# Context handed over turned, first query stacks taken straight from SBUF, and constant rows written by another engine

## The chip, the cores and the metric

The kernel runs on one core of one Trainium2 chip. The metric is the device time of one execution in microseconds (us). The engines are TensorE (PE, with its weight loads PEld), VectorE (DVE), ScalarE (ACT), GpSimd (POOL) and SyncE (SP), which here only issues DMAs; ACT issues a few as well.

## The reference, cut to what matters

A gated cross-attention block is followed by a mixture-of-experts block. There are B=8 batches of T=256 tokens with HID=512 features. The change touches the first half alone:

```python
# hidden = layernorm(x), ssm = ctx_2048, H=32 heads of D=16, HK=8 key heads, G=4
q = concat([ssm, hidden], -1) @ Wq          # 1024 -> 512
k, v = hidden @ Wk, hidden @ Wv             # 512 -> 128
sk, sv = ssm @ Wsk, ssm @ Wsv
scores = q . concat(sk, k) / 4 + alibi bias, masked to a window of 64 keys
x = x + tanh(g_xattn) * (softmax(scores) @ concat(sv, v)) @ Wo
```

## The kernel before, in words

All eight batches are worked through on the one core. Every float32 product is made as three fp32r products: a value is split into a high part (a copy by ACT, names ending in `_hi`) and a low part (value minus high part, names ending in `_lo`, by DVE or POOL), and `PASSES` multiplies hi.hi, lo.hi and hi.lo.

Attention is written as one software pipeline over `SLOTS`. A slot is one block of scores of one key head. A batch has 32 slots (`UNITS`), four to a group (key head) g. Each engine has its own instruction list for a slot, written out in a fixed order, and work of other batches is hung in at fixed offsets with `due(n, offset)`: an offset of -31 is slot 1 of the batch before.

For batch b the steps are: SP loads the rows of x and of the context (`load_rows`); DVE makes row statistics, POOL inverse roots (`x_roots`) and the normalised rows (by DVE for the first two batches). `prep(b, i)` turns 128 rows at a time with four TensorE transposes into a bank of `ps_proj`, i = 0, 1 for the context and 2, 3 for x; `prep_high` (ACT) and `prep_low` (DVE) split the turned block into `actT_hi`, `actT_lo`. `keys_values` and `queries` multiply these with the weights. The two banks of `ps_proj` are used in turn, in the order of `projections()`: a job waits (`take_bank`) until the job two before it has been emptied by DVE (`pj_done`). In the steady pipeline prep stands in slots 0 to 3, the key products in slots 5 and 6.

Scores are made from two stacks in SBUF, `k_stack` (KS) and `q_stack` (QS): their middle rows hold the three parts of keys and queries, their other rows constants for mask and bias, written once for each group by ACT (`key_rows_out`, `query_rows_out`, five instructions a group). Keys and queries reach the stacks through DRAM (`keep_k`, `keep_q`, then `stack_k`, `stack_q`); only for the first batch's groups 0 and 1 (`DIRECT`) do queries go from SBUF to SBUF (`stack_q_first`). `maxima` (DVE) takes row maxima, which are turned, copied and put into the query stack by a small DMA of ACT (`max_rows`); `scores_turned` then makes the turned scores 14 slots (`LAG`) after `scores`, ACT takes exponentials (`probsT`), and `times_v`, two DVE transposes, a POOL scaling (`o_normal`) and a product with Wo follow.

Before slot 0 stands an opening, written out by hand on each engine: the weights are loaded through an eight-part staging buffer (`weight(n)`, order `halves`: Wsk, four parts of Wq, Wk, four of Wq, Wsv, Wv, then four of Wo), split by ACT (`weights_high`) and by DVE or POOL (`weights_low`), and batch 0 is projected, with batch 1's keys. Batch 1's queries are made in slots 3, 6, 9 and 12 (`SECOND_Q`) and go into the same `qT` buffers, so that `q_high` of batch 1 waits for batch 0's `keep_q`. The probabilities lie over the staging buffer, so that `exponentials` of slot 18 waits for the last weight part.

After attention come router, shared expert and experts, which the change leaves alone.

Of the kernel before, what the change touches and what calls it, by code (L numbers as in the profile page):

```python
# [78 lines left out]
PREP, K_PROJ, Q_PROJ, V_PROJ = (-32, -31, -30, -29), (-27, -26), (-24, -22, -19, -16), (-7, -5)  # L79
# [7 lines left out]

DIRECT, FILL_ROWS, SECOND_Q = 2, {0: 3, 2: 4, 4: 5, 6: 6, 8: 7}, (3, 6, 9, 12)
# [33 lines left out]
def projections():  # L122


    order = [("prep", 0, i) for i in range(4)] + [("k", 0, 0)] + [("q", 0, r) for r in range(G)] + [("v", 0, 0)]
    order += [("prep", 1, i) for i in range(4)] + [("k", 1, 0)]
# [11 lines left out]
def build(nc, a, out):  # L138
# [21 lines left out]
    CTX = at("ctx_rows", 140 * KIB, [P, TB, HID])  # L160
# [5 lines left out]
    OT = {h: at(f"oT_{h}", (184 + n * 4) * KIB, [P, TB, HC, P], F32R) for n, h in enumerate(("hi", "lo"))}  # L166
    OB = at("o_blocks", 192 * KIB, [P, 2, T // 32, 2 * D])
# [87 lines left out]
    ones_set, tg_done, q_rows_set, k_rows_set = sem("ones_set"), sem("tg_done"), sem("q_rows_set"), sem("k_rows_set")  # L255
# [7 lines left out]
    k_in, max_in = ([sem(f"{n}_in{g}") for g in range(HK)] for n in ("k", "max"))  # L263
    q_in = [sem(f"q_in{p}") for p in range(PAIRED)]
    q_first = [sem(f"q_first{g}") for g in range(DIRECT)]
# [29 lines left out]
    ctx_t = a["ctx_2048"].rearrange("b (t p) d -> p b t d", p=P)  # L295
# [53 lines left out]
    def tile_columns(i):  # L349

        src, t = i // TB, i % TB
        return slice(None), slice(src * HC, (src + 1) * HC), slice(t * P, (t + 1) * P)
# [85 lines left out]
    def _(sp):  # L438
        sp.dma_start(CTX[:, 0], ctx_t[:, 0, 0]).then_inc(ctx_first, 16)
        sp.dma_start(CTX[:, 1], ctx_t[:, 0, 1]).then_inc(ctx_in, 16)  # L440

# [20 lines left out]
        def keep_q(b):  # L462
            sp.wait_ge(pj_done, passed("q", b, G - 1))
            for j, (part, _) in enumerate(PASSES):
                sp.dma_start(q_kept_d[b % 2, :, j], Q[part][:].rearrange("p i f r w -> p (i f r w)").bitcast(F32)
                             ).then_inc(q_kept, 16)

        def stack_k(b, g):
            sp.wait_ge(k_kept, 16 * PARTS * (b + 1))
            if b == 0:  # L470
                sp.wait_ge(pad_kept, 16)
                sp.wait_ge(k_rows_set, g + 1)
            else:
                sp.wait_ge(st_mm, (b - 1) * UNITS + NB * (g + 1))
            sp.dma_start(KS[DATA:FINE, g].rearrange("p i v w s -> p i (v w s)").bitcast(F32),
                         key_pairs(b % 2, g)).then_inc(k_in[g], 16)

        def stack_q_first(g):
            sp.wait_ge(pj_done, passed("q", 0, G - 1))
            sp.wait_ge(q_rows_set, 4 * (g + 1))  # L480
            for j, (part, _) in enumerate(PASSES):
                sp.dma_start(QS[DATA + j * D:DATA + (j + 1) * D, g].rearrange("p i f r w -> p (i f r w)").bitcast(F32),
                             Q[part][g * D:(g + 1) * D].rearrange("p i f r w -> p (i f r w)").bitcast(F32)
                             ).then_inc(q_first[g], 16)

        def stack_q(b, p):
            gs = slice(2 * p, 2 * p + 2)
            sp.wait_ge(q_kept, 16 * PARTS * (b + 1))
            if b == 0:
                sp.wait_ge(q_rows_set, 8 * (p + 1))  # L490
            else:
                sp.wait_ge(st_mm, (b - 1) * UNITS + 2 * NB * (p + 1))
# [24 lines left out]
        for p in range(DIRECT // 2, PAIRED):  # L517
            stack_q(0, p)
            for g in (2 * p, 2 * p + 1):
                stack_k(0, g)  # L520
            if p == DIRECT // 2:
                keep_k(1)
        for n in range(SLOTS):
# [42 lines left out]
            if s == 1:  # L566
                sp.wait_ge(q_kept, 16 * PARTS * B)
# [75 lines left out]
    def _(pool):  # L643
# [23 lines left out]

        def scale_outputs(n):
# [40 lines left out]

        link(pool.memset(half[:], -0.5))  # L710
        pool.memset(VA[:], 1.0).then_inc(ones_set, 1)
# [6 lines left out]
        for n in range(SLOTS):  # L718
            b = due(n, STATS[1] + 1, 2)
# [135 lines left out]
    def _(act):  # L855
# [4 lines left out]
        def key_rows_out(g):  # L860
            act.activation(KS[:, g].rearrange("p i v w s -> p i (v w) s"),
                           key_rows[:].rearrange("p v w -> p (v w)").unsqueeze(1).unsqueeze(3).broadcast_to(
                               [P, NB, 2 * W, 2]),
                           ACT.Copy).then_inc(k_rows_set, 1)

        def query_rows_out(g):
            for r in range(G):
                act.activation(QS[:, g, :, :, r, :],
                               onehot[:].rearrange("p (f w) -> p f w", f=2).unsqueeze(1).broadcast_to([P, NB, 2, HQ]),
                               ACT.Copy, scale=slopes[:, g, r:r + 1]).then_inc(q_rows_set, 1)  # L870

        def prep_high(b, i):
            act.wait_ge(prep_t, 4 * b + i + 1)
            act.activation(AT["hi"][tile_columns(i)], chunks(place("prep", b, i)), ACT.Copy).then_inc(prep_hi, 1)
# [8 lines left out]
        def q_high(b, r):  # L883
            if b >= 1 and r == 0:
# [1066 lines left out]
```

## Time and profile before

| | |
|---|---|
| median of 3 runs | 981.62 us (979.45 to 984.07) |
| the profiled execution's own time | 981.09 us |
| its span | 979.2 us |
| PE busy | 93% of the span |
| DVE, POOL, ACT busy | 58%, 49%, 42% |

The span is what the profile covers from the first to the last instruction; the execution's own time is 1.9 us longer. Busy shares are means over stages with different limits, so they don't tell by themselves which engine holds up the end.

### The profile page before, as it was taken

How to read it: one execution, taken by the hardware profiler on the slowest of the kernel's cores; microseconds unless marked ns; L12 is line 12 of the kernel's file. 1: busy time of each engine (PE TensorE's matmuls, PEld its weight loads, DVE VectorE, ACT ScalarE, POOL GpSimd, SP SyncE). 2: the span in 40 equal slices, each digit the busy share in tenths (PEclk: the TensorE clock that was granted, in tenths of full speed). 3: DMA queues.
4: the chain of work that ended last, by engine and by line, in shares of the span. 5: the costliest groups of instructions: out<-in, count | busy, mean ns of one | idle time of the engine just before them, and what ended most of it. 6: DMA issues, size and time to landing. Idle time of an engine off the chain costs nothing.

```text
span 979.2 us, 17727 instructions
## 1 busy us (share of the span) xinstructions
PE 911.4 (93%) x6744; PEld 778.0 (79%) x6744; DVE 568.9 (58%) x1123; ACT 408.4 (42%) x858; POOL 477.6 (49%) x525
## 2 busy tenths in 40 slices
PE   6869999999998999989998979889999999999998
PEld 6768989888888979777786857678888888888886
DVE  5447575766667574666223654855556565555657
ACT  4655444453535353454311423333444444344431
POOL 1123061513333150325122997726688887888841
PEclk9979999999999999999999989999999999999999
DMA  6695567474747464697010113441110201201026
GB/s 222 169 189 156 128 165 194 136 198 118 200 131 203 108 190 112 159 254 250 1 44 22 43 52 124 139 161 44 66 65 28 81 22 65 86 22 66 22 95 249
DMA packets 80422, 117.01 MB, mean 120 GB/s; under 512 B 6345, under 2 KB 49098, under 8 KB 79306
## 3 DMA queue, kind: packets, MB, share of 16 engines
q1 hardware_dynamic: 78592, 115.11, 41.3%
q8 instruction: 54, 0.88, 0.4%
q10 hardware_dynamic: 1746, 0.77, 0.4%
q14 instruction: 30, 0.25, 0.1%
HBM read 77.13 MB, written 37.81 MB: 117 GB/s over the span
## 4 chain that ended last, share of the span: by engine, by line
PE 75%; DVE 9%; POOL 6%; DMA 4%; issue 4%; ACT 2%; SPq 1%; ACTq 0%; DVEq 0%; POOLq 0%
PE ps_proj L1550 21%; PE ps_scores L1849 18%; PE ps_scoresT L1849 9%; PE ps_o L1661 5%; PE ps_scores L1629 4%; PE ps_proj L1849 4%; PE ps_scoresT L1648 4%; PE ps_scores L1550 3%; PE ps_scoresT L1550 2%; DMA q_stack<-max_rows 2%; DVE actT_lo L1185 2%; DVE neg_max L1220 2%; DVE o_blocks L1238 1%; DMA q_kept<-qT_hi 1%; PE ps_o L1550 1%
## 5 line engine op out<-in xcount | busy, mean ns | idle before, releaser
L1220 DVE TENSOR_REDUCE neg_max<-ps_scores 128x2 f32<-128x384 f32 (+1 forms) x256 | 128.8, 513 | 139.0 <-PE ps_scores L1629 137.1
L910 ACT ACTIVATE probsT<-ps_scoresT 128x512 f32<-128x512 f32 (+1 forms) x256 | 134.9, 542 | 144.7 <-PE ps_scoresT L1648 141.3
L1629 PE MATMUL ps_scores<-k_stack,q_stack 114*128 114x192 f32 (+1 forms) x512 | 105.4, 290 | 13.9 <-DVE neg_max L1220 9.2
L1108 ACT ACTIVATE part_sums<-ps_scores 128x512 f32<-128x512 f32 x96 | 57.4, 598 | 137.9 <-PE ps_scores L1849 137.9
L1648 PE MATMUL ps_scoresT<-q_stack,k_stack 116*128 116x256 f32 x448 | 104.2, 304 | 6.7 <-DMA q_stack<-max_rows 4.6
L1629 PEld LDWEIGHTS ps_scores<-k_stack,q_stack 114*128 114x128 f32 x512 | 81.0, 195 | 27.8 <-DVE neg_max L1220 17.9
L673 POOL TENSOR_TENSOR o_normal<-o_blocks,inv_sums 128x128 f32<-128x128 f32 x64 | 25.7, 402 | 147.0 <-DVE inv_sums L1240 147.0
L796 POOL TENSOR_TENSOR w_expert_lo<-w_sums,w_expert_hi 128x256 fp32r<-128x256 f32 x64 | 64.2, 1015 | 45.8 <-ACT w_expert_hi L1039 45.8
L808 POOL TENSOR_TENSOR big<-big,basis 128x512 f32<-128x512 f32 x56 | 77.5, 1401 | 14.9 <-DVE basis L1494 14.9
L1648 PEld LDWEIGHTS ps_scoresT<-q_stack,k_stack 116*128 116x128 f32 x448 | 71.6, 194 | 9.8 <-DMA q_stack<-max_rows 5.2
L679 POOL TENSOR_TENSOR oT_lo<-oT_raw,oT_hi 128x256 fp32r<-128x256 f32 x32 | 23.5, 736 | 111.2 <-ACT oT_hi L919 111.2
L1550 PE MATMUL ps_proj<-actT_hi,wq_hi 128*128 128x256 f32 x224 | 65.0, 290 | 0.0
L1550 PE MATMUL ps_proj<-actT_hi,wq_lo 128*128 128x256 f32 x224 | 64.2, 287 | 0.0
L1550 PE MATMUL ps_proj<-actT_lo,wq_hi 128*128 128x256 f32 x224 | 64.2, 287 | 0.0
L1485 DVE TENSOR_TENSOR basis<-part_sums,silu_gate 128x512 f32<-128x512 f32 x32 | 24.2, 756 | 68.3 <-ACT silu_gate L1116 68.3
L1661 PE MATMUL ps_o<-probsT,v_ones 128*32 128x128 f32 (+1 forms) x2048 | 63.3, 265 | 0.5 <-issue 0.5
L1661 PEld LDWEIGHTS ps_o<-probsT,v_ones 128*32 128x32 f32 x2048 | 52.8, 110 | 9.5 <-issue 1.0
L1494 DVE TENSOR_TENSOR basis<-basis,big 128x512 f32<-128x512 f32 x56 | 57.2, 1021 | 1.0
L796 POOL TENSOR_TENSOR w_expert_lo<-w_raw,w_expert_hi 128x256 fp32r<-128x256 f32 x48 | 46.2, 977 | 20.9 <-ACT w_expert_hi L1039 20.8
L1464 DVE TENSOR_TENSOR part_sums<-part_sums,ps_scoresT 128x512 f32<-128x512 f32 x32 | 22.0, 688 | 53.1 <-ACT part_sums L1108 53.1
L1849 PE MATMUL ps_scores<-sum_hi,w_expert_hi 128*128 128x512 f32 x128 | 50.1, 392 | 2.5 <-ACT part_sums L1108 2.5
L1849 PE MATMUL ps_scores<-xnT_hi,w_expert_hi 128*128 128x512 f32 x128 | 50.3, 393 | 0.0
(262 smaller groups left out, 2549.3 us busy)
## 6 DMA issues: line engine op xcount, KB each, us to landing
k_stack<-k_kept SPq DMA_DIRECT2D x64, 192.0 KB, 5.5
q_stack<-q_kept SPq DMA_DIRECT2D x31, 384.0 KB, 5.4
q_kept<-qT_hi SPq DMA_DIRECT2D x16, 512.0 KB
big<-coeff_rows SPq DMA_DIRECT2D x8, 1024.0 KB, 4.7
xn_rows<-in_x SPq DMA_DIRECT2D x8, 512.0 KB, 4.5
k_kept<-kT_hi SPq DMA_DIRECT2D x16, 256.0 KB
q_kept<-qT_lo SPq DMA_DIRECT2D x8, 512.0 KB
x_rows<-in_x SPq DMA_DIRECT2D x8, 512.0 KB, 5.4
```

The lines of the kernel that those rows point to most:

```text
L673: pool.tensor_tensor(ON[:, p % 2, :, odd * D:(odd + 1) * D], OB[:, n % 2, :, 0:D], RI[:, n % 2].unsqueeze(2).broadcast_to([P, T // 32, D]) ...
L796: pool.tensor_tensor(WS[n % 2]["lo"][:, w, :], w_source(n, w), WS[n % 2]["hi"][:, w, :].bitcast(F32), ALU.subtract).then_inc(e_lo, 1)
L808: pool.tensor_tensor(dst, dst, BS[:, j, :], ALU.add).then_inc(acc_done, 1)
L910: act.activation(PT[:, g % 2, 2 * j:2 * j + blocks].rearrange("p h f r w -> p (h f r w)"), ST[:, n % 2, 0:blocks].rearrange("p h n -> p (h ...
L1108: act.activation(TP[:, u % 2, j, :], src[:, u % 2, :], ACT.Copy).then_inc(taken, 1)
L1220: dve.tensor_reduce(NM[:, g % 2, 2 * i:2 * i + 2], SA[:, n % 2, :, 0:keys], AX.X, ALU.max, negate=True).then_inc(max_done, 1)
L1494: dve.tensor_tensor(dst, BS[:, j, :], cB[:, k % 2, group_columns(t)], ALU.mult).then_inc(basis_done, 1)
L1550: ins = pe.matmul(out, stat(s, c), mov(m, c), start=c == cs[0] and j == 0, stop=c == cs[-1] and j == PARTS - 1)
L1629: ins = pe.matmul(SA[:, n % 2, f, 0:2 * (near.stop - near.start)], QS[0:TOP, g, i, f].rearrange("p r w -> p (r w)"), keys[:, near, :].rear ...
L1648: ins = pe.matmul(ST[:, n % 2, v, :], KS[0:ROWS, g, j + v, 1 - v].rearrange("p w s -> p (w s)"), QS[0:ROWS, g, j + v].rearrange("p f r w - ...
L1661: ins = pe.matmul(PO[32 * r:32 * r + 2 * D, j * W:j * W + cols_j], VA[:, j, g, :], PT[:, n % 2, 2 * j:2 * j + cols_j // W, :, r, :].rearra ...
L1849: ins = pe.matmul(bank[:, u % 2, :], WS[n % 2][s][:, w, c * P:(c + 1) * P], operand(MEETS[w], m, c, g), start=first and c == 0 and j == 0, ...
```

## The change

1. The context is passed already turned: on the host it is laid out as (batch, 128 partitions, 4 chunks, 256 tokens). `CTX` holds it turned, and the transposes and PSUM copies of `prep(b, 0..1)` are gone. ACT splits it from SBUF in two halves (`ctx_high`, slots 29 and 30 of the batch before), and the low part is made by POOL (`ctx_low`, slots 30 and 31) for batches 2 to 7, by DVE for batches 0 and 1. `prep` is left for x alone, in slots 1 and 3. The first key product no longer waits for `prep`.
2. All eight groups of the first batch take their queries straight from SBUF; batch 0 has no `keep_q` and no `stack_q`. Batch 1's queries go into buffers of their own (`Q1`, over `oT_hi`/`oT_lo`).
3. The constant rows of both stacks are written by POOL (`rows_out`), not by ACT, all before slot 0 in POOL's list.
4. The opening has a new order: x is loaded earlier, Wsk is loaded by ACT's queue, `keep_k(0)` stands before the loads of Wsv and Wv, the Wo loads and `keep_k(1)` stand after group 3's stacks, and seven matmuls on ones (`warm`) come first on PE.

```diff
-PREP, K_PROJ, Q_PROJ, V_PROJ = (-32, -31, -30, -29), (-27, -26), (-24, -22, -19, -16), (-7, -5)
+CTX_HIGH, CTX_LOW = (-35, -34), (-34, -33)
+PREP, K_PROJ, Q_PROJ, V_PROJ = (-31, -29), (-27, -26), (-24, -22, -19, -16), (-7, -5)
-DIRECT, FILL_ROWS, SECOND_Q = 2, {0: 3, 2: 4, 4: 5, 6: 6, 8: 7}, (3, 6, 9, 12)
+SECOND_Q, SPLIT_WO = (3, 6, 9, 12), 9
+FIRST_STACK, WARM = 16 * (1 + PARTS), 7
...
+    Q1 = {h: at(f"second_qT_{h}", (184 + n * 4) * KIB, [P, NB, 2, G, HQ], F32R) for n, h in enumerate(("hi", "lo"))}
...
         def load_rows(b):
-            sp.wait_ge(prep_t, 4 * b)
+            sp.wait_ge(prep_t, TB * b)
             sp.dma_start(XN[:], x_t[:, b]).then_inc(x_in, 16)
+            sp.wait_ge(ctx_lo, 2 * b)
             sp.dma_start(CTX[:], ctx_t[:, b]).then_inc(ctx_in, 16)
...
-        for n in range(FIRST_O):
+        for n in range(1, FIRST_O):
             weight(n)
-            if n == 2:
-                sp.dma_start(XN[:], x_t[:, 0]).then_inc(x_in, 16)
+            if n == FIRST_O - 3:
+                keep_k(0)
         load_rows(1)
-        keep_k(0)
-        for n in range(FIRST_O, len(halves)):
-            weight(n)
-        for g in range(DIRECT):
+        for g in range(HK):
             stack_k(0, g)
             stack_q_first(g)
-        keep_q(0)
-        for p in range(DIRECT // 2, PAIRED):
-            stack_q(0, p)
-            for g in (2 * p, 2 * p + 1):
-                stack_k(0, g)
-            if p == DIRECT // 2:
+            if g == 3:
+                for n in range(FIRST_O, len(halves)):
+                    weight(n)
                 keep_k(1)
...
+        def rows_out(g):
+            if g == 0:
+                pool.wait_ge(consts_in, 48)
+            pool.tensor_copy(KS[:, g].rearrange("p i v w s -> p i (v w) s"),
+                             key_rows[:].rearrange("p v w -> p (v w)").unsqueeze(1).unsqueeze(3).broadcast_to(
+                                 [P, NB, 2 * W, 2])).then_inc(rows_set, 1)
+            for r in range(G):
+                pool.tensor_scalar(QS[:, g, :, :, r, :],
+                                   onehot[:].rearrange("p (f w) -> p f w", f=2).unsqueeze(1).broadcast_to([P, NB, 2, HQ]),
+                                   slopes[:, g, r:r + 1], None, ALU.mult).then_inc(rows_set, 1)
+
+        def ctx_low(b, j):
+            pool.wait_ge(ctx_hi, 2 * b + j + 1)
+            pool.tensor_tensor(AT["lo"][ctx_half(j)], CTX[ctx_half(j)], AT["hi"][ctx_half(j)].bitcast(F32),
+                               ALU.subtract).then_inc(ctx_lo, 1)
...
+        rows_out(0)
         x_roots(0)
+        rows_out(1)
         weights_low(HALF_V[0])
         weights_low(HALF_V[1])
         x_roots(1)
+        for g in range(2, HK):
+            rows_out(g)
         for n in range(FIRST_O, len(halves)):
             weights_low(n)
...
+        def ctx_high(b, j):
+            if b == 0:
+                act.wait_ge((ctx_first, ctx_in)[j], 16)
+            else:
+                act.wait_ge(ctx_in, 16 * (b + 1))
+                act.wait_ge(v_mm, 2 * b - 1)
+            act.activation(AT["hi"][ctx_half(j)], CTX[ctx_half(j)], ACT.Copy).then_inc(ctx_hi, 1)
...
         def q_high(b, r):
-            if b >= 1 and r == 0:
-                act.wait_ge(q_kept, 16 * PARTS * b)
+            if b == 2 and r == 0:
+                first_stacked(act)
+            elif b >= 3 and r == 0:
+                act.wait_ge(q_kept, 16 * PARTS * (b - 1))
...
+        def warm():
+            ones = VA[:, 0].rearrange("p g e -> p (g e)")
+            pe.wait_ge(ones_set, 1)
+            for _ in range(WARM):
+                pe.matmul(PJ[:, 1, 0:T], ones[:, 0:P], ones[:, 0:T], start=True, stop=True)
```

ACT's opening list becomes: Wsk high, both context halves high, weights 1 to 5 high, `prep_high(0, 0..1)`, weight 6 high, `k_high(0)`, weights 7 to 11 high (10 and 11 are Wsv and Wv), then `q_high(0, 0..3)`. DVE's becomes: weight 0 low, both context halves low, weight 1 low, statistics of batch 0, weights 2 and 3 low, `normalise(0)`, weights 4 and 5 low, `prep_low(0)`, weight 6 low, `k_low(0)`, weights 7 to 9 low, `q_low(0)`, statistics of batch 1, and so on.

## Rows read from the trace of the kernel before

**Rows 1.** The page: busy time of each engine, and engines on the final chain.

```profile
PE 911.4 (93%) x6744; PEld 778.0 (79%) x6744; DVE 568.9 (58%) x1123; ACT 408.4 (42%) x858; POOL 477.6 (49%) x525
...
PE 75%; DVE 9%; POOL 6%; DMA 4%; issue 4%; ACT 2%; SPq 1%; ACTq 0%; DVEq 0%; POOLq 0%
```

**Rows 2.** Busy time by stage: from:to, length, each engine, clock, DMA share, GB/s.

```profile
40.00:75.00 35.00, 24.85 (x182) 22.84 (x184) 15.34 (x40) 20.70 (x44) 5.19 (x5) 0.82 0.79 183
...
130.00:460.00 330.00, 308.48 (x3474) 276.95 (x3473) 214.20 (x555) 150.60 (x342) 109.61 (x172) 0.99 0.66 176
```

**Rows 3.** PE's waits, 110 to 440 us: total us, times, longest us.

```profile
PE ps_proj L1550 <- DVE actT_lo L1185: 6.6, 5, 1.3
...
PE ps_proj L1573 <- DVE xs_lo L1263: 3.0, 5, 0.6
```

**Rows 4.** Final chain in one steady batch, and the same piece one batch later.

```profile
198.54 0.56 DVE xs_lo L1263
199.10 0.46 DVE neg_max L1220
...
252.81 0.56 DVE xs_lo L1263
```

**Rows 5.** PE timeline of those slots: start, length, instruction, [idle before, releaser].

```profile
197.61 0.60 PE L1573 MATMUL ps_proj<-ident,ctx_rows 128*128 128x128 f32 x4
197.97 0.45 PE L1629 MATMUL ps_scores<-k_stack,q_stack 114*128 114x192 f32 x2
...
204.95 0.36 PE L1550 MATMUL ps_proj<-actT_hi,wkv_hi 128*128 128x256 f32 x1 [1.32 <-DVE actT_lo L1185]
```

**Rows 6.** POOL's groups by form: busy us, mean ns of one.

```profile
L697 POOL TENSOR_SCALAR x_normal<-x_rows,x_mean_var,x_rstd 128x512 f32<-128x512 f32 x16 | 33.2, 2082 | 1.5 <-POOL x_rstd L658 1.4
...
L702 POOL TENSOR_TENSOR wo_lo<-w_stage,wo_hi 128x512 fp32r<-128x512 f32 x4 | 5.0, 1280 | 30.7 <-ACT wo_hi L858 30.7
...
L711 POOL MEMSET v_ones<- 128x1024 f32 x1 | 1.0, 952 | 0.1
```

**Rows 7.** Final chain through the opening.

```profile
22.60 0.72 PE ps_scores L1603 x6
...
39.53 10.74 DMA q_kept<-qT_hi
...
50.74 5.67 DMA k_stack<-k_kept
...
63.27 8.86 DMA q_stack<-max_rows
```

**Rows 8.** SP's timeline of the opening.

```profile
32.88 0.65 SPq L475 DMA_DIRECT2D k_stack<-k_kept  x1
33.63 0.63 SPq L482 DMA_DIRECT2D q_stack<-qT_hi  x1
...
60.43 0.59 SPq L453 DMA_DIRECT2D xn_rows<-in_x  x1
```

**Rows 9.** DVE's timeline, 71 to 73 us.

```profile
71.92 0.69 DVE L1168 BATCH_NORM_STATS2 stats<-xn_rows 128x6 f32<-128x512 f32 x1 [0.69 <-DMA xn_rows<-in_x]
```

**Rows 10.** PE's timeline at slot 0 of batch 0.

```profile
40.03 0.59 PE L1629 MATMUL ps_scores<-k_stack,q_stack 114*128 114x128 f32 x4
```

**Rows 11.** POOL's timeline: first and last of the six instructions of `x_roots(1)`.

```profile
26.49 0.23 POOL L653 TENSOR_SCALAR var_eps<-mean_var 128x2 f32<-128x2 f32 x1
...
28.42 0.19 POOL L658 TENSOR_TENSOR rstd<-rstd,tmp 128x2 f32<-128x2 f32 x1
```

**Rows 12.** DMA issues up to 40 us: KB each, median us from issue to landing.

```profile
w_stage<-in_L_xattn_Wo SPq DMA_DIRECT2D x4, 256.0 KB, 6.5
...
w_stage<-in_L_xattn_Wsv SPq DMA_DIRECT2D x1, 256.0 KB, 3.6
```

**Rows 13.** Landing of the three loads of x issued before 75 us.

```profile
DMA to landing us min/median/max: 3.9/6.0/11.5
```

**Rows 14.** POOL's timeline, slot 32 of a steady batch.

```profile
198.62 0.40 POOL L673 TENSOR_TENSOR o_normal<-o_blocks,inv_sums 128x128 f32<-128x128 f32 x1 [1.94 <-DVE inv_sums L1240]
```

More of the change, by code:

```diff
@@ L718, in _ @@
         for n in range(SLOTS):
+            for j in range(2):
+                b = due(n, CTX_LOW[j], 2)
+                if b is not None:
+                    ctx_low(b, j)
             b = due(n, STATS[1] + 1, 2)
@@ L858, in weights_high, with prep_high @@
             act.activation(halves[n][1]["hi"], staged(n), ACT.Copy).then_inc(weights_hi, 1)
[L860 to L874, printed above, removed]
+        def ctx_high(b, j):
[5 more added lines that the diff above has]
+            act.activation(AT["hi"][ctx_half(j)], CTX[ctx_half(j)], ACT.Copy).then_inc(ctx_hi, 1)
+        def prep_high(b, t):
+            act.wait_ge(prep_t, TB * b + t + 1)
+            act.activation(AT["hi"][tile_columns(t)], chunks(place("prep", b, t)), ACT.Copy).then_inc(prep_hi, 1)
         def k_high(b):
@@ L976, in _ @@
         for n in range(SLOTS):
-            for i in range(4):
+            for i in range(2):
+                b = due(n, CTX_HIGH[i], 2)
+                if b is not None:
+                    ctx_high(b, i)
                 b = due(n, PREP[i] + 1, 2)
@@ L1274, in shared_times @@
             times(q, hT[:, n, group_columns(t)])
-        prep_low(0, 0)
-        prep_low(0, 1)
         weights_low(0)
+        ctx_low(0, 0)
+        ctx_low(0, 1)
         weights_low(1)
-        row_stats(0, 0)
-        row_stats(0, 1)
-        weights_low(2)
-        weights_low(3)
-        normalise(0, 0)
-        normalise(0, 1)
-        for n in range(4, 7):
-            weights_low(n)
-        prep_low(0, 2)
-        prep_low(0, 3)
+        for t in range(TB):
+            row_stats(0, t)
+        for n in range(2, 4):
+            weights_low(n)
+        for t in range(TB):
+            normalise(0, t)
+        for n in range(4, 6):
+            weights_low(n)
+        for t in range(TB):
+            prep_low(0, t)
+        weights_low(6)
+        k_low(0)
         for n in range(7, BY_DVE):
             weights_low(n)
-        k_low(0)
-        row_stats(1, 0)
-        row_stats(1, 1)
         for r in range(G):
             q_low(0, r)
-        normalise(1, 0)
-        normalise(1, 1)
+        for t in range(TB):
+            row_stats(1, t)
+        for j in range(2):
+            ctx_low(1, j)
         v_out(0)
-        for i in range(4):
-            prep_low(1, i)
+        for t in range(TB):
+            normalise(1, t)
+        for t in range(TB):
+            prep_low(1, t)
         k_low(1)
@@ L1314, in _ @@
                 o_back_turn(m // 2)
-            for i in range(4):
-                b = due(n, PREP[i] + 1, 2)
+            for t in range(TB):
+                b = due(n, PREP[t] + 1, 2)
                 if b is not None:
-                    prep_low(b, i)
+                    prep_low(b, t)
             b = due(n, K_PROJ[1] + 1, 2)
@@ L1588, in keys_values, with keys, values @@
             return product(dst[:, src * T:(src + 1) * T], lambda h, c: WKV[h][:, m + src, c, :],
-                           lambda h, c: AT[h][:, src * HC + c, :], range(HC))
+                           lambda h, c: AT[h][:, src * HC + c, :], range(HC), before)
+        def keys(b, src):
+            ins = keys_values("k", b, src)
+            if src == 1:
+                ins.then_inc(k_mm, 1)
+        def values(b, src):
+            keys_values("v", b, src).then_inc(v_mm, 1)
         def queries(b, r):
@@ L1714, in shared_gate_up @@
             gate_up(q, (SHARED + n) % 2, t)
-        pe.wait_ge(ident_in, 16)
-        prep(0, 0)
-        prep(0, 1)
-        keys_values("k", 0, 0)
+        warm()
+        keys(0, 0)
         first_queries(range(HC))
-        prep(0, 2)
-        prep(0, 3)
-        keys_values("k", 0, 1).then_inc(k_mm, 1)
+        for t in range(TB):
+            prep(0, t)
+        keys(0, 1)
         first_queries(range(HC, 2 * HC))
-        for src in range(2):
-            ins = keys_values("v", 0, src)
-        ins.then_inc(v_mm, 1)
-        for i in range(4):
-            prep(1, i)
-        for src in range(2):
-            ins = keys_values("k", 1, src)
-        ins.then_inc(k_mm, 1)
+        for i in range(2):
+            values(0, i)
+        for t in range(TB):
+            prep(1, t)
+        for i in range(2):
+            keys(1, i)
         for n in range(SLOTS):
@@ L1757, in _ @@
                     queries(b, i)
-            for src in range(2):
-                b = due(n, V_PROJ[src], 1)
+            for i in range(2):
+                b = due(n, V_PROJ[i], 1)
                 if b is not None:
-                    ins = keys_values("v", b, src)
-                    if src == 1:
-                        ins.then_inc(v_mm, 1)
+                    values(b, i)
             b = due(n, TURN_V)
```

175 lines of the change are left out of this document (84 added, 91 removed).

## The prediction

> **What bounds the kernel now.** I read the page first, for the shares: PE is busy 93% of the span, no other engine over 58%, and three quarters of the final chain is PE's [rows 1]. So PE time and PE stalls count, and work moved between other engines counts only where PE waits for it. The busy time by stage then shows where PE has room: in 40 to 75 us it is busy 24.9 of 35 us, in the 330 us of steady attention 308.5 [rows 2]. Everything after 460 us is the experts, which the change leaves alone.
>
> For the steady stage I read PE's waits. Two of them belong to the turning of context and x: 6.6 us in five waits for `actT_lo` and 3.0 us in five for `xs_lo`, thus 1.3 and 0.6 us in each batch [rows 3]. The chain says why: from 198.54 us, in slots 0 to 4, it goes through DVE, four `prep_low` between maxima and transposes, until the first key product can start at 204.95 [rows 4, 5]. The pattern comes back 54.3 us later [rows 4], once for each of batches 2 to 7, six times.
>
> For the opening I read the chain again. It runs from the query products into a 10.7 us round trip of `q_kept` through DRAM, then a `k_stack` load of 5.7 us and a `max_rows` DMA of 8.9 us [rows 7]. That seems to promise 10 us and more. But DVE's timeline has a gate behind it: the statistics of batch 2 stand in slot 18 of DVE's list and start at 71.92 us, released by the landing of x, which SP issued at 60.43 because it comes to that load only after all stacks of batch 0 [rows 8, 9]. What the opening is worth is how much earlier that gate opens, not how long the DRAM trip was.
>
> **Steady batches, the transposes.** Eight of 16 transposes a batch go. Four cost about 0.4 us of PE: those at 197.61 are followed by the next scores at 197.97 [rows 5]. That is 0.8 us a batch, on PE's own path.
>
> The two context `prep_low` leave DVE, 0.5 to 0.7 us each, of which the chain shows one kind at work between the maxima [rows 4]. I replay slots 0 to 5 from the point where nothing has changed, the end of `xs_lo` at 199.10. DVE: maximum to 199.57, maximum and the first x low part to 200.6, maximum and `oT_raw` to 201.5, the two small halves to 202.0, maximum, transpose, reciprocal to 203.0, second x low part to 203.6. PE: scores of slot 3 at 199.6, `times_v` to 201.0, second transposes to 201.45, slots 4 and 5 to 202.25. There the context key product can start, because its operands were ready in slot 31; it lasts 1.45 us (12 matmuls at 0.12, six in 0.72 [rows 7]), slot 6 follows, and the x key product starts at 204.3, after the low part's 203.6. So the first key product moves from 204.95 to 202.25: 2.7 us a batch, which contains the transposes (0.8), the waits (1.3 and 0.6), all once. Six batches: 16.2 us. Bounds: if only the transposes count, 0.8 x 6 = 5; if the whole of the DVE run of two low parts came on top, 3.0 x 6 = 18.
>
> What goes in. ACT's two copies a batch only change place and source. POOL gets two subtractions a batch, 128x512 each, 1.28 us at the nearest row [rows 6]. They stand in slots 30 and 31, ahead of `o_normal` of slot 32, which POOL began at 198.62 [rows 14]; with them it starts near 199.3 and ends at 199.7, and DVE needs it after 200.04. The cover is 0.3 us; if it is gone, `o_back_turn` slips by as much, and the second x low part behind it has 0.7 us to spare before the x key product. Cost nothing, bound 0.5 x 6 = 3 us. SP's new wait for `ctx_lo` stands in front of a context load some 6 slots after that low part: nothing.
>
> **Opening up to slot 0.** Wsk and the context land at about 5 us, so the first key product can start near 7 us. What follows it gains less. I put the statistics of batch 0 at 11 us, since DVE waits for weight 1 behind x; POOL reaches `x_roots(0)` only after `rows_out(0)`. With c for the POOL time of one group's rows (below) and constants landed at 8 us, that is max(11, 8 + c), then 2.1 to 2.8 us for the roots [rows 11], normalise 1, weight 4's low part 0.7, twelve matmuls, transposes, split, Wk product: the second half of the query products starts at 21.4 for c = 3.7, against 22.6 [rows 7]. The seven matmuls of `warm` stand in time that PE idles; an early clock helps little because PE waits for DVE there. I take 0 for them, bounds -1 and +1.
>
> Then the order costs something. `keep_k(0)` waits for `k_low(0)`, about 22.7, and Wsv and Wv stand behind its three issues of 0.65 us (the length of a `k_stack` issue [rows 8]): issued at 24.8 and 25.3, where DMA then also carries three writes, x and the context. The nearest landings are 3.6 us on an idle machine and 6.5 us for Wo behind the same writes [rows 12]; I take 6. On ACT the four `q_high` are queued behind the splits of Wsv and Wv, so `q_low` ends at 34; on POOL two low parts of 1.28 us [rows 6]; on PE `values(0)` waits till 33, 5.7 us idle, and would then run at the lower clock, as after the waits of 40 to 75 us, where the granted clock is 0.82 of full [rows 2]. `x_roots(1)` ends at T0 = 38.4, the keys of batch 1 at 44: slot 0 moves from 40.0 [rows 10] to 44, 4 us later. This is hidden if the gate of slot 18 is later still.
>
> **The constant rows, c.** The trace has no POOL copy or single multiply of this size. A group is one copy of 1024 columns and four multiplies of 256. From below: memset, 0.95 us for 1024 columns, thus 0.93 a thousand and about 1.0 + 4 x 0.4 = 2.6 us. From above: the two-operation `TENSOR_SCALAR`, 2.08 us for 512, 3.7 ns a column: 4.0 + 4 x 1.1 = 8.5 us [rows 6]. A one-operation multiply should cost about half of the two-operation one, 0.65, and the copy, which computes nothing, lies by the memset, 1.1: c = 3.7 us. I take that.
>
> The Trainium skill bears on this (GPSIMD Engine Reference, Engine selection): one-input operations on GpSimd run at roughly line rate, only two-input ones are about twice as slow as VectorE. By an estimate from that page's 128 elements a cycle, c would be near 2.7. The trace doesn't bear it out for the one-input row it has, 2.08 us for 512 columns [rows 6]; by that row's rate the sum would be 8.5.
>
> **The gate of slot 18.** POOL ends rows 2 to 7 at T0 + 6c = 60.6, and SP follows each with four issues, 2.5 us [rows 8]. SP alone would need, from group 2 on, 6 x 2.5 and four Wo loads and `keep_k(1)`, 4 us, thus nearly as much. `load_rows(2)` is issued at 38.4 + 22.2 + 2.7 = 63.3, against 60.43. Landing took 11.5 us then, the slowest of three loads, 6.0 is their median [rows 13]; 1.5 MB of `q_kept` writes and 1.15 MB of reads are gone and 1.15 MB from SBUF to SBUF come in, so I take 7.5: 70.8, against 71.92, 1 us gained. The second gate, the last Wo low part that `exponentials` of slot 18 wants, is at 60.6 + 5.1 = 65.7 and stays below. PE's own way (slot 0 at 44, four query products of 2.9 us, the maxima) reaches slot 18 near 65, also below. Removing `q_kept` thus gives 1 us of its 10.7: the stall passes to POOL's rows and SP's queue. Bounds: c = 2.6, T0 earlier and a landing of 5 give -6; c = 8.5 gives 43 + 51 + 3 + 7 = 104, thus +32.
>
> **Sum.** 981.1 (the profiled execution, 0.5 below the median of 981.6) - 16.2 - 1 = 963.9; 1 us back for part of POOL's bound: 965.
>
> **Rivals.**
> *POOL's rows become the bound (slower).* Place: `rows_out(2..7)`, in front of SP's stacks and, through SP's list, of the load for slot 18. Each 0.17 us of c beyond 3.7 is 1 us; the steady gain is used up when the gate is 17 us later, at c near 6.4. With c = 8.5: 981 - 16 + 32 = 997. For it: the 2.08 us row. Against: memset's row, and that a single multiply does half the work. 0.10.
> *POOL's rows cost in between*, c = 4.5 to 6: gate 5 to 14 us later, 970 to 979. 0.17.
> *The steady gain is refilled.* DVE and `o_normal` give back half, or denser DMA traffic (share 0.66 now [rows 2]) makes `max_rows` late: 8 us instead of 16, 972. For it: that DMA took 8.9 us in the crowded opening. Against: it is issued seven slots before it is wanted. 0.13.
> *The opening pays as its chain promises*: PE at slot 19 by 65, 957. For it: fewer bytes. Against: SP's issue time. 0.15.
> *The forecast*, 960 to 969: 0.45.
>
> **Chances.** A measurement of this kernel can tell about 0.5%, 4.9 us, from no change. Below 976.7: forecast, the refill, the good opening and two thirds of the middle case, 0.85. Within 0.5%: the rest of the middle case and rows that cost between it and c = 7.3, 0.07. Slower: c beyond that, and what I overlook, 0.08. Range 954 to 978, which leaves the costly rows and the far ends out.
>
> **What would show it.** Steady period 54.3 down to 51.6 us, no wait for `actT_lo` or `xs_lo` before the key products; first scores near 44 us; POOL groups of rows at 3.7 us; statistics of batch 2 near 71 us, released by x. Wrong if: the period stays over 53 (step "steady"), POOL's multiply is over 1 us (step "c"), or slot 18 waits for something else than x's landing.

## The result, and the profile after

The changed kernel takes 991.51 us (median of 4 runs, 988.84 to 992.69), the one before beside it 981.29: a ratio of 1.0104, 95% interval 1.0079 to 1.0129. It is 10 us slower; 965 was forecast, in a range of 954 to 978. The profiled execution took 990.86 us with a span of 989.0.

The page after, busy time of each engine (before: [rows 1]):

```profile
PE 916.6 (93%) x6694; PEld 780.7 (79%) x6694; DVE 573.2 (58%) x1111; ACT 388.1 (39%) x818; POOL 530.5 (54%) x578
```

The page has 50 matmuls fewer for TensorE, and yet it is busy 5 us longer. The busy time by stage of the kernel after says in which stages (from:to, length, each engine, clock, DMA share, GB/s; before: [rows 2]):

```profile
0.00:40.00 40.00, 24.27 (x142) 21.57 (x142) 13.07 (x22) 11.81 (x21) 15.12 (x25) 0.92 0.50 158
40.00:75.00 35.00, 29.20 (x187) 27.78 (x187) 16.54 (x39) 7.72 (x18) 32.93 (x40) 0.80 0.58 130
...
130.00:460.00 330.00, 310.24 (x3383) 276.85 (x3381) 212.06 (x536) 146.43 (x333) 117.61 (x176) 0.96 0.63 168
```

In the steady 330 us TensorE is as busy as before, although 48 transposes have gone (eight in each of six batches), and its clock is 0.96, not 0.99. From 40 to 75 us POOL is busy 32.9 of 35 us, where it had 5.2.

**The steady stage.** TensorE's waits of the kernel after, 110 to 440 us (before: [rows 3]):

```profile
PE ps_scores L1670 <- DVE neg_max L1250: 12.1, 17, 1.0
PE ps_proj L1583 <- POOL oT_lo L702: 3.1, 6, 0.5
```

The two waits of [rows 3] are gone, as forecast, and the scores now wait 12.1 us for row maxima. Slot 0 of a steady batch shows why. POOL's timeline of the kernel after, then VectorE's and TensorE's at the same time (start, length, instruction, [idle before, releaser]):

```profile
202.96 2.50 POOL L688 TENSOR_TENSOR actT_lo<-ctx_turned,actT_hi 128x512 fp32r<-128x512 f32 x2
```

```profile
203.26 1.01 DVE L1257 CAST max_halves<-neg_max 128x8 fp32r<-128x8 f32 x1
204.30 1.18 DVE L1259 TENSOR_TENSOR max_halves<-neg_max,max_halves 128x8 fp32r<-128x8 f32 x1
205.41 0.41 DVE L1250 TENSOR_REDUCE neg_max<-ps_scores 128x2 f32<-128x256 f32 x1
```

```profile
205.88 0.47 PE L1670 MATMUL ps_scores<-k_stack,q_stack 114*128 114x192 f32 x2 [0.98 <-DVE neg_max L1250]
...
207.49 0.47 PE L1670 MATMUL ps_scores<-k_stack,q_stack 114*128 114x192 f32 x2 [0.78 <-DVE neg_max L1250]
```

VectorE's two `max_halves` instructions work on 8 columns; their medians in this kernel are 0.17 us. Here they take 1.01 and 1.18 us, and they end at 204.27 and 205.48, when POOL's two subtractions end (half of the 2.50 us, 1.25, is one of them: 202.96 + 1.25 = 204.21, and 205.46). The next maximum stands behind them, and TensorE behind the maximum. TensorE's clock then falls. Busy time by stretches of 1 us of the kernel after (the clock is the third number from the end):

```profile
204.00:205.00 1.00, 0.89 (x8) 0.65 (x7) 0.96 (x2) 1.00 (x4) 1.00 (x2) 1.00 0.30 41
205.00:206.00 1.00, 0.12 (x1) 0.13 (x2) 1.00 (x3) 0.53 (x2) 0.46 (x1) 1.00 0.04 10
206.00:207.00 1.00, 0.71 (x5) 0.43 (x5) 0.96 (x4) 0.36 (x1) 0.40 (x1) 1.00 0.60 186
207.00:208.00 1.00, 0.51 (x3) 0.51 (x4) 1.00 (x3) 0.38 (x2) 0.00 (x0) 0.92 0.21 86
208.00:209.00 1.00, 1.00 (x15) 0.73 (x18) 1.00 (x3) 0.54 (x1) 0.00 (x0) 0.50 0.97 365
209.00:210.00 1.00, 1.00 (x26) 0.79 (x16) 0.64 (x3) 0.48 (x2) 0.37 (x1) 0.50 1.03 309
210.00:211.00 1.00, 1.00 (x9) 0.99 (x6) 0.00 (x0) 0.00 (x0) 0.35 (x1) 0.50 0.93 266
```

From 205 to 208 it was busy 1.34 of 3 us; the three microseconds behind them run at 0.50, the level of 1.2 GHz. TensorE waits 0.98 and 0.78 us behind two instructions of 0.17 us each; the second wait is 0.46 in experiment 2, which has no such stretch, so that about 1.3 us are theirs. The clock costs 1.5 more, half of 3; together that is 2.8 of the 3.1 us between this kernel's period and experiment 2's. The final chain repeats it one batch later (kernel after):

```profile
203.26 1.02 DVE max_halves L1257
...
258.08 1.04 DVE max_halves L1257
```

That is a period of 54.8 us, where 54.3 stood [rows 4] and 51.6 was forecast. A small piece of this stood in the kernel before already: in the same place its cast and its subtraction took 0.14 and 0.59 us, the subtraction to the end of POOL's `oT_lo`. Its timelines:

```profile
202.54 0.75 POOL L679 TENSOR_TENSOR oT_lo<-oT_raw,oT_hi 128x256 fp32r<-128x256 f32 x1 [3.52 <-ACT oT_hi L919]
202.72 0.59 DVE L1229 TENSOR_TENSOR max_halves<-neg_max,max_halves 128x8 fp32r<-128x8 f32 x1
```

**The opening.** POOL's timeline of the kernel after, start of the constant rows (before, `x_roots(0)` had ended by 13.8):

```profile
9.51 1.04 POOL L678 CAST k_stack<-key_rows 128x1024 fp32r<-128x1024 f32 x1 [7.77 <-DMA slopes<-in_slopes]
10.63 4.29 POOL L682 TENSOR_SCALAR q_stack<-onehot,slopes 128x256 fp32r<-128x256 f32 x4
15.00 0.23 POOL L658 TENSOR_SCALAR var_eps<-mean_var 128x2 f32<-128x2 f32 x1
```

The final chain of the kernel after, from there to the gate of slot 18 (before: [rows 7, 9]):

```profile
31.78 7.03 DMA w_stage<-in_L_xattn_Wv
...
40.91 2.95 PE ps_proj L1583 x12
...
49.57 5.20 PE ps_proj L1583 x24
...
76.57 2.04 DVE max_halves L1257
...
80.66 0.69 DVE stats L1193
```

The first scores stand in TensorE's timeline, the load of x for batch 2 in SP's (before: [rows 8, 10]):

```profile
54.59 0.59 PE L1670 MATMUL ps_scores<-k_stack,q_stack 114*128 114x128 f32 x4
```

```profile
76.22 0.58 SPq L466 DMA_DIRECT2D xn_rows<-in_x  x1
```

Slot 0 starts at 54.6, not at 44; the statistics of batch 2 at 80.7, not at 70.8. The opening has long small instructions too: the 2.04 us of `max_halves` above end at 78.6, when POOL's four subtractions for Wo end (73.58 to 78.57). By 147.9 us, the first `xs_lo`, the kernel is 6.1 us behind the one before (141.8).

### The profile page after: what moved, and what is told of

Same layout as the page of the kernel before. It is cut to its first block, busy times and chain, and to the rows that moved or that the text cites. A ratio compares the mean times of both kernels' runs of the same rounds, so it can differ in the third digit from the quotient of the medians.

```text
span 989.0 us, 17636 instructions
## 1 busy us (share of the span) xinstructions
PE 916.6 (93%) x6694; PEld 780.7 (79%) x6694; DVE 573.2 (58%) x1111; ACT 388.1 (39%) x818; POOL 530.5 (54%) x578
## 4 chain that ended last, share of the span: by engine, by line
PE 76%; DVE 7%; POOL 7%; issue 4%; ACT 3%; DMA 2%; SPq 0%; ACTq 0%; DVEq 0%; POOLq 0%
PE ps_proj L1583 22%; PE ps_scores L1882 18%; PE ps_scoresT L1882 9%; PE ps_o L1702 5%; PE ps_scores L1670 5%; PE ps_scoresT L1689 4%; PE ps_proj L1882 4%; PE ps_scores L1583 3%; PE ps_scoresT L1583 2%; DVE neg_max L1250 2%; DMA q_stack<-max_rows 1%; ACT probsT L937 1%; PE ps_proj L1609 1%; DVE max_halves L1257 1%; DVE o_blocks L1268 1%
## 5 line engine op out<-in xcount | busy, mean ns | idle before, releaser
L1702 PE MATMUL ps_o<-probsT,v_ones 128*32 128x128 f32 (+1 forms) x2048 | 66.8, 275 | 0.5 <-issue 0.5
L1702 PEld LDWEIGHTS ps_o<-probsT,v_ones 128*32 128x32 f32 x2048 | 55.5, 115 | 10.4 <-issue 2.1
L1882 PE MATMUL ps_scores<-sum_hi,w_expert_lo 128*128 128x512 f32 x128 | 50.3, 393 | 0.0
```

The source lines that it names most:

```text
L1702: ins = pe.matmul(PO[32 * r:32 * r + 2 * D, j * W:j * W + cols_j], VA[:, j, g, :], PT[:, n % 2, 2 * j:2 * j + cols_j // W, :, r, :].rearra ...
L1882: ins = pe.matmul(bank[:, u % 2, :], WS[n % 2][s][:, w, c * P:(c + 1) * P], operand(MEETS[w], m, c, g), start=first and c == 0 and j == 0, ...
```

## The experiments

Times are medians; ratios, with their 95% intervals, stand against runs of the kernel before on the same chip: 980.69 us for the first four, 982.11 for the next four, 980.34 for the last three. A gain or a cost in us is against the changed kernel's 991.5 where nothing else is said; as the kernel before itself gave 980.3 to 982.1 in these series, a difference between two series is uncertain by 1 to 2 us.

**1. The low part of the context by VectorE again**, for all batches, before `prep_low`:

```diff
         for n in range(SLOTS):          # GpSimd
-            for j in range(2):
-                b = due(n, CTX_LOW[j], 2)
-                if b is not None:
-                    ctx_low(b, j)
         for n in range(SLOTS):          # VectorE, in front of prep_low
+            for j in range(2):
+                b = due(n, CTX_LOW[j], 2)
+                if b is not None:
+                    ctx_low(b, j)
```

> The changed kernel, with the context's low parts of batches 2 to 7 made by VectorE in slots 30 and 31 where GpSimd made them. Theory A (shared port): the two small max_halves operations of slot 0, 1.01 and 1.18 us in the changed kernel's trace, take that long only because a GpSimd subtraction with SBUF operands runs beside them; without it they fall back to 0.17 us each, TensorE's two waits for neg_max (0.98 and 0.78 us) and the half clock at 208 to 211 us go, and the batch period falls from 54.8 to 51.5-52.8 us: 12 to 18 us faster than the changed kernel, 973 to 980. Rival B (ScalarE): the two ctx_high copies ahead of xs_hi make VectorE late; they are unchanged, so the period stays at 54 to 55 and the time at 989 to 993. Rival C (VectorE is simply full in slots 0 to 4): two more operations on VectorE make it worse, period 55 or more.

Measured: 979.65 us, 0.9981 (0.9964 to 0.9998), 11.9 below the changed kernel. The period is 52.2 us, and the wait for `neg_max` 7.2 us in 12. With more work on the engine that the stall was charged to, the long waits are gone: VectorE was held up, not overloaded.

**2. The same subtraction left on GpSimd, three slots later.**

```diff
-CTX_HIGH, CTX_LOW = (-35, -34), (-34, -33)
+CTX_HIGH, CTX_LOW = (-35, -34), (-31, -30)
```

> The changed kernel, with GpSimd's context low parts of batches 2 to 7 three slots later (slots 1 and 2 of the next batch, not 30 and 31), between the small max_halves operations of slot 0 and slot 4. Same engine, same work. Theory A (shared port): the max_halves of slot 0 take 0.17 us again, period 51.5 to 53.5, 973 to 983 us. If what counts is GpSimd's load or its lateness with o_normal, and not the meeting with max_halves: no gain, or the stall moves to max_halves of slot 4, period 54 to 55. Rival B (ScalarE): 989 to 993.

Measured: 977.27 us, 0.9965 (0.9951 to 0.9980), 14.2 below the changed kernel. No engine does less; only the place differs. Its final chain has the period that was forecast (51.7 us), and its waits are halved:

```profile
203.79 0.29 DVE xs_lo L1293
255.50 0.29 DVE xs_lo L1293
```

```profile
PE ps_scores L1670 <- DVE neg_max L1250: 5.6, 12, 0.5
```

Its clock is 1.00 in each microsecond from 203 to 212.

**3. ScalarE's copies of the context three slots earlier**, against the reading that these copies delay ScalarE and through it the split of x:

```diff
-CTX_HIGH, CTX_LOW = (-35, -34), (-34, -33)
+CTX_HIGH, CTX_LOW = (-38, -37), (-34, -33)
```

> The changed kernel, with ScalarE's two ctx_high copies of batches 2 to 7 three slots earlier (slots 26 and 27), away from xs_hi; GpSimd's low parts stay. Rival B: the chain from probsT over actT_hi and xs_hi to xs_lo is 1.2 us shorter, period 52 to 53.5, 977 to 985 us. Theory A: the small max_halves operations still meet the GpSimd subtraction; they start some 1 us earlier and last until it ends, period 54 to 55, 987 to 993 us.

Measured: 990.82 us, 1.0093 (1.0074 to 1.0113); the wait for `neg_max` is 12.2 us in 17, as in the changed kernel. The rival fell.

**4. The loads of Wsv and Wv ahead of `keep_k(0)`**, as they stood before the change:

```diff
         for n in range(1, FIRST_O):
             weight(n)
-            if n == FIRST_O - 3:
-                keep_k(0)
+        keep_k(0)
         load_rows(1)
```

> The changed kernel, with keep_k(0) behind the loads of Wsv and Wv in SyncE's list (it stood before them); nothing else. In the changed kernel's trace these loads are issued at 30.4 and 31.8 us, land at 38.8, and ScalarE's four q_high and GpSimd's two low parts wait behind them. Theory D (opening order): now they land by 20 us, q_high runs at about 30, the values of batch 0 follow the query products without a gap, and slot 0 moves from 56.5 to 46 to 50 us; the time falls by 4 to 9 us to 982 to 987, the rest being limited by the last rows of GpSimd, as T0 + 6 x 4.58 us moves with T0 from 45.3 to about 38. Rival: GpSimd's rows or the load of x for slot 18 take the gain, and less than 2 us is left (989 to 992).

(Slot 0 of the changed kernel starts at 54.6; the 56.5 of this text is slot 2.) Measured: 988.36 us, 1.0078 (1.0052 to 1.0104), 3.1 gained, less than the 4 to 9 expected and more than the rival's 2. The intervals of this ratio and of the changed kernel's (1.0079 to 1.0129) overlap, so the times alone don't secure it; the traces have slot 0 at 51.3 and the statistics of batch 2 at 77.4, both 3.3 us earlier. The final chain of this kernel shows what stands next: the load of x, now behind `keep_k`, and then the constant rows, one group after the other, up to SP's stacks and the next load of x:

```profile
30.71 7.26 DMA xn_rows<-in_x
...
42.33 0.98 POOL k_stack L677
43.31 3.86 POOL q_stack L681 x4
47.17 0.98 POOL k_stack L677
48.15 3.60 POOL q_stack L681 x4
...
66.52 3.62 POOL q_stack L681 x4
...
72.74 4.61 DMA xn_rows<-in_x
```

**5. Three edits together**: 2, 4, and `x_roots(0)` in front of `rows_out(0)` in POOL's list.

```diff
-        rows_out(0)
         x_roots(0)
+        rows_out(0)
         rows_out(1)
```

> The changed kernel with three reorderings together: GpSimd's context low parts in slots 1 and 2 of the next batch (as in the run that took the stall of max_halves away), keep_k(0) behind the loads of Wsv and Wv, and x_roots(0) ahead of rows_out(0) in GpSimd's list. Theory D (opening order), additive: 991.5 - 14.2 (measured for the first) - 3.1 (measured for the second) - 3.7 for the third, because x_roots(0) started at 15.0 us behind the rows of group 0 in the changed kernel's trace while its statistics were there about 11.2: 970.5, range 968 to 973. Rival F (the rows of groups 2 to 7 and the load of x behind them are a fixed end): the third gives under 1.5 us, 973 to 976, because x_roots(1), from which the rows start, hangs on x's second load and not on the first batch's normalisation.

Measured: 968.87 us, 0.9865 (0.9837 to 0.9893); slot 0 at 48.1. The gains of 2 and 4 add up to 17.3; 22.6 came, so that the roots, which had waited for 5.4 us of rows, are worth up to 5.3. The edit was not run alone.

**6. The same, with the rows of groups 2 and 3 in POOL's idle time** (16.0 us before the split of Wsv in the changed kernel):

```diff
         rows_out(1)
+        rows_out(2)
         weights_low(HALF_V[0])
         weights_low(HALF_V[1])
+        rows_out(3)
         x_roots(1)
-        for g in range(2, HK):
+        for g in range(4, HK):
             rows_out(g)
```

> The kernel of the three reorderings, and GpSimd writes the rows of group 2 before the low parts of Wsv and Wv and those of group 3 before x_roots(1), in time in which it sat idle (22.7 to 38.7 us in the changed kernel's trace). Theory F' (the rows are the bound of the opening): the last rows are ready 2 x 4.58 us earlier, and the load of x for slot 18 with them; TensorE's own way, which has slot 17 only some 2 us before that load lands, then takes over, so 2 to 5 us less than with the three alone. Rival: TensorE's way is already the bound there, under 1 us less.

Measured: 966.80 us, 0.9845 (0.9815 to 0.9874), 2.1 better: less than the 9.2 us of rows that moved. Slot 0 is later (50.1), the statistics of batch 2 earlier (72.8 after 74.2); neither is more than single executions of one opening differ by (2 us, see the sum below). The final chain there no longer goes through the rows' end but through a `max_rows` DMA of 6.67 us issued at 70.20.

**7. As 5, with the rows written by ScalarE**, groups 0 and 1 in front of `q_high(0, ..)`, 2 and 3 around `prep_high(1, ..)`, 4 to 7 in slots 0, 2, 4 and 6:

```diff
-        rows_out(0)
-        rows_out(1)
...
-        for g in range(2, HK):
-            rows_out(g)
...
+        rows_out(0)
+        rows_out(1)
         for r in range(G):
             q_high(0, r)
...
+            if n in (0, 2, 4, 6):
+                rows_out(4 + n // 2)
```

> The kernel of the three reorderings, with all constant rows written by ScalarE again (groups 0 and 1 ahead of q_high of batch 0, 2 and 3 among the high parts of batch 1, 4 to 7 in slots 0, 2, 4 and 6). Before the change a group took ScalarE 1.05 us and four times 0.50 us (some 2.8 us from start to end), GpSimd takes 4.58 us. Theory F': as the run with spread rows, 2 to 5 us less than with the three alone. If writing rows on GpSimd was no loss: the same time, or longer, because ScalarE's q_high wait behind the rows.

Measured: 964.50 us, 0.9819 (0.9792 to 0.9847), 4.4 below 5. What one group costs each engine is read from the groups by form, first of the changed kernel, then of this one (busy us, mean ns of one):

```profile
L682 POOL TENSOR_SCALAR q_stack<-onehot,slopes 128x256 fp32r<-128x256 f32 x32 | 30.9, 981 | 0.1
```

```profile
L903 ACT ACTIVATE q_stack<-onehot,slopes 128x256 fp32r<-128x256 f32 x32 | 13.6, 497 | 0.0
L898 ACT ACTIVATE k_stack<-key_rows 128x1024 fp32r<-128x1024 f32 x8 | 8.4, 1046 | 0.0
```

The copy costs the same on both; the multiply costs POOL twice as much. SP comes to the load of x for batch 2 at 64.3; in 5 it came at 69.7, in the changed kernel at 76.2. The gate of slot 18 gives way to another DMA, as in 6; this kernel's final chain:

```profile
67.94 6.99 DMA q_stack<-max_rows
```

**8. Without the seven matmuls of `warm`.**

```diff
-        warm()
         keys(0, 0)
```

> The changed kernel without the seven matmuls on ones; nothing else. In its trace the first query products run at full clock at 9.7 us, but TensorE then waits for VectorE's weight low parts until 19.7 us and is at half clock from 20.2 us anyway. Theory: within 1 us of the changed kernel, 990 to 992.5. Rival (the early clock is worth its place): 2 us or more slower; or (the warm matmuls delay the first key product): 1 us or more faster.

Measured: 991.03 us, 1.0100 (1.0067 to 1.0134): no difference to the changed kernel that this can tell.

**9. The suspected cost twice.** The subtraction stays where experiment 2 put it, and GpSimd does it once more in slots 30 and 31 (`dup` is a semaphore on which only the real subtraction waits, on the same engine):

```diff
 on top of 2:
+            for j in range(2):
+                b = due(n, CTX_HIGH[j] + 1, 2)
+                if b is not None:
+                    pool.wait_ge(ctx_hi, 2 * b + j + 1)
+                    pool.tensor_tensor(AT["lo"][ctx_half(j)], CTX[ctx_half(j)], AT["hi"][ctx_half(j)].bitcast(F32),
+                                       ALU.subtract).then_inc(dup, 1)
```

> The low part of the context stays in slots 1 and 2 as in the second experiment, but for batches 2 to 7 GpSimd also does the same two subtractions once more in slots 30 and 31, into the same place, which nothing reads before slot 1. Only the suspected cost is added: no other engine has more to do. Theory A (two GpSimd subtractions beside the two small max_halves instructions of VectorE hold these up, and TensorE's maxima with them): the stall comes back, a max_halves instruction of over 1 us in most batches, period near 54.8 us, time 986 to 993. Rival (the gain of the second experiment came from somewhere else that its new place changed, such as the context load behind ctx_lo or o_normal): 975 to 980, period 51.7.

Measured: 991.47 us, 1.0111 (1.0091 to 1.0132). Nothing needs the added result before slot 1, and it costs 14.2 us over experiment 2. The timelines of this kernel, POOL's and VectorE's:

```profile
202.35 2.51 POOL L753 TENSOR_TENSOR actT_lo<-ctx_turned,actT_hi 128x512 fp32r<-128x512 f32 x2
```

```profile
202.64 1.02 DVE L1265 CAST max_halves<-neg_max 128x8 fp32r<-128x8 f32 x1
203.69 1.19 DVE L1267 TENSOR_TENSOR max_halves<-neg_max,max_halves 128x8 fp32r<-128x8 f32 x1
```

From 208 to 210 the granted clock is 0.50 here too.

**10. Fills in place of the repeated subtractions.** They write the same place and read nothing; zeros stand there until the real low part is written.

```diff
 on top of 2:
+            b = due(n, CTX_HIGH[1] + 1, 2)
+            if b is not None:
+                pool.wait_ge(ctx_hi, 2 * b + 1)
+                for i in range(3):
...
+                    pool.memset(AT["lo"][:, 0:HC, :].bitcast(F32), 0.0).then_inc(dup, 1)
```

> As the run before, but instead of the two repeated subtractions GpSimd fills the same place (128x1024) with zeros three times, about 0.95 us each, thus 2.9 us in slots 30 and 31 of instructions that read no SBUF. It tells what about GpSimd's work holds VectorE up. If any GpSimd instruction does it: the first max_halves instruction waits to the end of one fill, up to 0.95 us, the second as well, time 980 to 990. If only reading of SBUF does it: max_halves stays near 0.2 us, time 975 to 980. In between (only the first of the two, the one with one input, waits): 977 to 984.

Measured: 978.91 us, 0.9977 (0.9963 to 0.9992). POOL is occupied longer at that place than in 9 (2.98 us for 2.51), and 12.6 of the 14.2 us are not there. This kernel's timelines:

```profile
202.64 2.98 POOL L756 MEMSET actT_lo<- 128x1024 f32 x3
```

```profile
202.93 0.68 DVE L1267 CAST max_halves<-neg_max 128x8 fp32r<-128x8 f32 x1
203.65 0.17 DVE L1269 TENSOR_TENSOR max_halves<-neg_max,max_halves 128x8 fp32r<-128x8 f32 x1
```

The cast, with one input, ends when the first fill ends (202.64 + 0.99 = 203.63). The subtraction, with two inputs, runs beside the second fill in its usual 0.17 us. The stall is 0.5 us, and the clock stays at 1.00. The in-between answer held.

**11. As 7, with batch 1's load of x ahead of `keep_k(0)`.**

```diff
-        keep_k(0)
         load_rows(1)
+        keep_k(0)
```

> The version with the constant rows by ScalarE, and batch 1's load of x and of the context issued before keep_k(0), not behind it. In that version x landed at 34.0 after 7.8 us, the inverse roots followed at once, and the keys of batch 1 and slot 0 behind them. Theory (x is still late): x lands 2 to 4 us earlier, slot 0 near 44, time 961 to 964. Rival (the writes of keep_k, now 1.3 us later, hold up the first stacks, or the gate is the max_rows DMA and SP's order behind it): 964 to 967, no gain.

Measured: 961.54 us, 0.9812 (0.9788 to 0.9836), the lowest median of all, 18.8 below the kernel before. 7 was 17.6 below the kernel before of its own series and the two intervals overlap, so the times don't tell how much of the 3.0 us between them is real; in the traces the statistics of batch 2 start at 66.5, not at 70.6. SP issues x at 18.4, slot 0 starts at 42.4 (46.4 in 7), and batch 1's keys, 24 matmuls, take this long in its final chain:

```profile
39.39 3.15 PE ps_proj L1596 x24
```

In the changed kernel the same 24 took 5.20, at 49.57; the granted clock there (49 to 55 us) is 0.56, here (38 to 43 us) 1.00.

## Why the prediction was wrong

**What bounds the kernel; transposes and low parts of x.** Right. Waits for `actT_lo` and `xs_lo` are gone, and the slots replayed from [rows 4, 5] were right in size: with the collision removed (experiment 2) the period is 51.7 us for the forecast 51.6. Between the first and the last `xs_lo`, five batches, experiment 2 is 12.9 us shorter than before (260.7 for 273.6); five times 2.7 is 13.5.

**The step that failed, "what goes in": POOL's two subtractions, "cost nothing, bound 0.5 x 6 = 3 us".** They cost 14.2 us (991.5 against 977.3), almost five times the bound, shown by moving them (2), by doubling them (9) and by giving them to VectorE (1, 11.9 us net of its own work). I asked what was queued behind them on POOL, `o_normal`, and found 0.3 us of cover. What they delayed was VectorE, by no semaphore: its two `max_halves` instructions ended only when POOL's subtractions did. In the period this takes back the whole steady gain (54.8 us, before 54.3). The rival "the steady gain is refilled" had the direction, by other mechanisms, VectorE and `o_normal`, or a late `max_rows`, and half the size.

The Trainium skill states the rule that I passed over (SBUF — State Buffer, Who interferes with whom): VectorE and GpSimd share one pair of ports, held for the whole instruction by whoever starts first; a VectorE copy or cast in its two-port mode contends with any GpSimd instruction, one with two SBUF inputs only with a GpSimd instruction that reads SBUF. The traces agree on both halves: the cast stretched from 0.17 to 0.68 us beside a fill that reads nothing and to 1.02 beside a subtraction, the two-input one to 1.19 beside the subtraction and not at all beside the fill. The kernel before showed it too: the two-input instruction took 0.59 us beside `oT_lo` in slot 0 of five steady batches, and the longest `max_halves` were 1.34 and 1.21 us. The prediction's replay of these slots gave the two 0.5 us together and didn't ask why they were longer than 0.17 each.

**The opening: "1 us gained".** Measured 8.7 us lost at the gate (80.7 against 71.9). The steps:
- *c = 3.7 us for a group's rows.* Measured 4.6 (0.98 for the copy, 3.6 for four multiplies). The copy lay by memset's row, as taken. "A one-operation multiply should cost about half of the two-operation one" failed: 0.90 us for 256 columns is 3.5 ns a column, against 4.1 in the two-operation row [rows 6], which the prediction's upper bound took as 3.7, and 2.5 assumed. Rows 2 to 7 took 28.3 us (45.30 to 73.58) where 22.2 were reckoned, 6.1 late: six times 0.9, and 0.7 in the first group, whose copy took 1.50 us. The rival "in between" (c = 4.5 to 6) had the size of c, and this error alone would give about 971, near its lower end, 970.
- *T0 = 38.4.* The last root of batch 1 ended at 45.3, 6.9 late. Two parts can be told. `rows_out(0)` held `x_roots(0)` until 15.0, where 11.7 was reckoned, because the constants landed at 9.4 and not at 8 and c was longer (5: up to 5.3 us). Beside the next copy of rows VectorE's normalisation of batch 0 then took 1.84 us for 1.00 before; whether POOL held it up too was not tested. Wsv and Wv came to SP at 30.4 and not at 24.8, because `k_low(0)` ended at 28.4 and not at 22.7, and landed at 38.8, 7.0 us after the issue where 6 was taken (4: 3.1 us).
- *Slot 0 at 44.* It came 10.6 us late, the 6.9 of T0 and 3.7 behind it: TensorE had waited for Wsv and Wv and was at half clock (0.50 from 38 to 43 us), so that batch 1's keys took 5.2 us.
- *Landing of x for batch 2, 7.5 us.* Measured 4.4, 3.1 less. The issue came 12.9 us late, 6.9 from T0 and 6.1 from the rows, so that x landed at 80.6, 9.8 later than forecast. VectorE came to the statistics at 80.65, behind a maximum; the 2.04 us of `max_halves` before it therefore cost nothing at this gate.
- *`warm`, 0.* Right (8).

Of the prediction's own three signs of being wrong the first came, a period over 53 us. POOL's multiply took 0.98 us in the mean, just under the 1 us named, and x's landing and the end of VectorE's queue met at slot 18.

Sum: of the 26.5 us between 965 and 991.5, the collision in the steady stage is 14.2 (2, 9). The other 12.3 are the distance of experiment 2 from the forecast, and they are the opening's: in its trace the statistics of batch 2 start at 82.5, 11.7 later than forecast, and the five batches behind are shorter by what was forecast to within 0.6. Of that the runs give back 3.1 (4), 5.3 more (5) and 4.4 more (7), 12.8 together; how they would add up singly, where they overlap, stays open. At the first `xs_lo` the changed kernel is 2 us ahead of experiment 2 (147.9 against 149.9), and so it is at slot 0 already (54.6 against 56.5), before any instruction that was moved. From 23 to 27 us the granted clock is 0.93 in its profiled execution and 0.50 in that of experiment 2: single executions of the same opening differ by this much, and a shift of under 2 us of one instruction between two traces shows little by itself.

The chance of slower, 0.08, named c and "what I overlook". Two errors of over 10 us in one direction, neither of them c alone, had no rival.

## What to carry to other kernels

Before work is moved to GpSimd, look at what VectorE does in the same microseconds, not only at what is queued behind it on GpSimd: two tiny instructions on the way to TensorE were worth 14 us, and three slots later the same work cost nothing that could be seen. An instruction of 8 columns that lasts 1 us in a timeline, with no wait before it, is the sign. In an opening, ask for each wait of a new order what it does to the load issued behind it; small misplacements of 3 to 5 us in this one added up, and undone together they made a version that beats both (961.5 us).

## What was not expected of the hardware

- A GpSimd subtraction of 1.25 us held up an 8-column VectorE instruction to its very end; beside a GpSimd fill only the cast was held up (0.68 us), the two-input subtraction ran in 0.17.
- A GpSimd multiply by a per-partition scalar takes 0.90 to 0.98 us for 256 columns, and its plain copy 0.98 us for 1024; on ScalarE the two take 0.50 and 1.05.
- The stretch of 3 us in slot 0 in which TensorE was busy 1.34 us was followed by 3 us at 1.2 GHz; in experiments 2 and 10, without the two long instructions, the clock stayed at 2.4 GHz there.
